# Attention one step deeper, projection heads prepared early, x's low part ahead of the angles, and attention's result read out by VectorE

## What is computed

```
q, k, v = x Wq', x Wk', x Wv'              # 32 query heads, 8 key/value heads, 128 wide
q, k = rope(rmsnorm(q)), rope(rmsnorm(k))  # positions: cache length + token
k_all = [16 cache pages of 32 keys, k];  v_all likewise   # 544 keys per sequence
p = softmax(q k_all' / sqrt(128), keys of the cache beyond its length masked)
o = p v_all;   u = o Wo'                   # 4096 -> 512
x1 = x + (causal convolution of u with a state-space kernel) + D u
out = x1 + ffn(cond(x1))                   # LoRA linear, then a gated low-rank expert layer
```

## Time and profile before

| what | value |
|---|---|
| median of 3 executions | 1270.46 us (1269.95 to 1273.42) |
| the profiled execution | 1272.64 us, span 1270.7 us |
| PE busy | 1234.1 us, 97% |
| PEld, DVE, ACT, POOL busy | 81%, 64%, 64%, 59% |
| mean granted clock of TensorE | 0.999 |
| attention of the two halves | about 166 to 482 us and 797 to 1113 us |

### The profile page before, as it was taken

One profiled execution on the slowest core, in us unless ns is written; L12 is line 12 of the kernel. 1 busy time (PEld: TensorE's weight loads), 2 busy tenths in 40 slices (PEclk: granted clock), 3 DMA queues, 4 the chain that ended last, 5 costly groups with the idle time before them and its releaser, 6 DMA issues.

```text
span 1270.7 us, 28683 instructions
## 1 busy us (share of the span) xinstructions
PE 1234.1 (97%) x7378; PEld 1033.0 (81%) x7378; DVE 810.5 (64%) x1725; ACT 809.2 (64%) x2258; POOL 753.3 (59%) x884
## 2 busy tenths in 40 slices
PE   6999999999999998999999999999999999999998
PEld 5778888899989986866777888888899998978756
DVE  5876666766766777962339766666676776655422
ACT  5676677778888874432336666778787888653320
POOL 3444467888888884433223433778888888754330
PEclk9999999999999999999999999999999999999999
DMA  6343288999999955406144242899999999434300
GB/s 229 123 134 119 96 229 227 227 232 242 237 234 234 233 139 180 145 1 199 42 161 138 96 153 90 243 217 234 226 241 239 224 234 241 108 115 145 91 32 34
DMA packets 147978, 214.82 MB, mean 169 GB/s; under 512 B 24949, under 2 KB 119479, under 8 KB 142136
## 3 DMA queue, kind: packets, MB, share of 16 engines
q1 hardware_dynamic: 130568, 204.86, 59.8%
q10 hardware_dynamic: 17328, 9.04, 2.4%
HBM read 203.33 MB, written 10.49 MB: 168 GB/s over the span
## 4 chain that ended last, share of the span: by engine, by line
PE 77%; SPq 10%; DVE 4%; issue 4%; ACT 2%; DMA 2%; ACTq 0%; DVEq 0%
PE PS L1106 14%; PE PS L1074 7%; PE PS L969 5%; PE PS L975 5%; PE PS L971 5%; PE PS L1171 4%; PE PS L1162 4%; PE PS L1168 4%; SPq L479 4%; SPq L464 4%; PE PS L1116 4%; PE PS L1213 2%; PE PS L955 2%; PE PS L1039 2%; PE PS L1041 2%
## 5 line engine op out<-in xcount | busy, mean ns | idle before, releaser
L622 POOL TENSOR_TENSOR kv_parts<-kv,k_hi 128x544 fp32r<-128x544 f32 x192 | 258.2, 1345 | 46.7 <-ACT k_hi L798 42.8
L1106 PE MATMUL PS<-probT,kv 128*128 128x128 f32 x2048 | 271.2, 275 | 5.2 <-DMA kv<-in_vpages 3.7
L1106 PEld LDWEIGHTS PS<-probT,kv 128*128 128x128 f32 x2048 | 248.8, 192 | 7.2 <-issue 5.9
L582 POOL TENSOR_TENSOR ring_parts<-ring,kv_parts 128x512 fp32r<-128x512 f32 x96 | 127.1, 1328 | 214.9 <-ACT kv_parts L685 186.8
L1594 DVE COPY probT<-PS 128x512 f32<-128x512 f32 x256 | 175.5, 686 | 3.1 <-PE PS L1074 3.1
L839 ACT ACTIVATE ring<-ring,smin 128x544 f32<-128x544 f32 x192 | 143.7, 748 | 39.4 <-DVE smin L1588 37.8
L1588 DVE CUSTOM_DVE_ANT_0 ring<-PS,mask,rq 128x544 f32<-128x544 f32 x192 | 149.8, 780 | 21.0 <-PE PS L1062 13.7
L798 ACT ACTIVATE k_hi<-kv 128x544 fp32r<-128x544 f32 x192 | 125.9, 657 | 56.8 <-PE PS L1062 50.5
L644 POOL TENSOR_TENSOR ring_parts<-ring,kv_parts 128x512 fp32r<-128x512 f32 x64 | 86.2, 1352 | 99.1 <-ACT kv_parts L894 99.1
L610 POOL TENSOR_SCALAR ring<-ring,rinv 128x512 f32<-128x512 f32 x192 | 133.3, 694 | 0.0
L1627 DVE TENSOR_TENSOR qo_parts<-qo,kv_parts 128x512 fp32r<-128x512 f32 x64 | 86.6, 1362 | 58.0 <-ACT kv_parts L896 55.2
(11 more groups left out here) (219 smaller groups left out, 2782.4 us busy)
## 6 DMA issues: line engine op xcount, KB each, us to landing
kv<-in_kpages SPq DMA_DIRECT2D x512, 128.0 KB, 2.6
kv<-in_vpages SPq DMA_DIRECT2D x512, 128.0 KB
ring<-in_w SPq DMA_DIRECT2D x44, 1024.0 KB, 5.1
v_new<-kv ACTq DMA_DIRECT2D x16, 256.0 KB, 4.3
k_new<-kv ACTq DMA_DIRECT2D x16, 256.0 KB, 2.3
kv<-k_new SPq DMA_DIRECT2D x32, 128.0 KB, 2.4
kv<-v_new SPq DMA_DIRECT2D x32, 128.0 KB
kv<-in_xT SPq DMA_DIRECT2D x8, 256.0 KB, 5.2
```

Of the source, the lines that this page charges most:

```text
L622: nc.gpsimd.tensor_tensor(kbuf_lo(par)[:, :, g, :], kbuf(par)[:, :, g, :], k_hi[:, e % 2, :].rearrange("p (j t) -> p j t", t=PSIZE), ALU.s ...
L1106: mm = nc.tensor.matmul(PS[:, at:at + D], vbuf(bpar)[:, c, gg * D:(gg + 1) * D], probT[:, g % 2, c * P:(c + 1) * P], start=(c == 0 and a = ...
```

## The change

Four edits, in five engines' streams.
- Attention's order gets one step deeper: `turn_probs` of g-3 and `values` of g-4 in step g, `turn_new` in steps 2 and 6, `values_new` in steps 0 and 4 of the next group, `v_free` in step 5 instead of 4, and the tail of the half accordingly. `spread_new` moves to steps 2 and 6.
- `keep_o` moves from ScalarE (steps 0, 4) to VectorE (steps 2, 6), and in the tail behind the last probT copies.
- The first two weights of the projection of the result and its first two heads are split by ScalarE around the last `spread_new`; the first 16 heads wait for one `keep_o` fewer. Weight block 14 is loaded before the last `o_done`, ahead of the small vectors.
- `prologue` is cut into `positions` and `angles`, and x's last low part is made between them. PE no longer waits for the sine ahead of block 1, but for the angles ahead of its tile 2 and for the sine ahead of tile 3 (their banks). On ScalarE the sine moves behind the stores of two value tiles and half of block 2, the rest of which now stands ahead of the first squares, in both halves.

```
 load_w(h, 15)
+sp.wait_ge(new_turned, QUADS * (h + 1))
+load_w(h, 14)                                  # was behind the small vectors
 sp.wait_ge(o_done, QUADS * (h + 1))
...
+for m in range(2, TILES): store_v(0, m)        # ScalarE, was behind the sine
+for c in range(2): upper(2, c)
 with act.If(h < 1):
     act.wait_ge(ang_ready, 1)
     ... Sin, Sin
+for c in range(2, KC): upper(2, c)
 for n in range(KU):
-    upper(2 + n // TILES, n % TILES)
+    if n >= TILES: upper(3, n % TILES)
     squares(n)
...
-if g % GU == 1 and not (first and g < GU):     # ScalarE, attention step
+if g % GU == 2 and not (first and g < GU):
     spread_new(b if g > GU else b - 1, int(g < GU))
-if g % GU == 0 and not first:
-    keep_o(b - 1, g // GU)
...
+upper_w(0); upper_w(1); upper_o(0)             # ScalarE, end of attention
 spread_new(HB - 1, 1)
+upper_o(1)
...
-pe.wait_ge(trig_ready, 2)                      # PE, ahead of block 1
...
-if g == GU and not first: mm.then_inc(v_free, 1)
+if g == GU + 1 and not first: mm.then_inc(v_free, 1)
...
 scores(b, par, g, first)                       # PE, attend
-if not (first and g < 2): turn_probs(b, g - 2, first); turn_new at g == 5, 1
+if not (first and g < 3): turn_probs(b, g - 3, first); turn_new at g == 6, 2
-if not (first and g < 3): values(b, par, g - 3, first)
+if not (first and g < 4): values(b, par, g - 4)
-if g == 7: values_new(b, par, 0, first)
-elif g == 3 and not first: values_new(b - 1, 1 - par, 1, False)
+if g == 0 and not first: values_new(b - 1, 1 - par, 0)
+elif g == 4 and not first: values_new(b - 1, 1 - par, 1)
...
 lower_x(0, range(3))                           # VectorE
-prologue()
+positions()
 lower_x(0, range(3, KC))
+angles()
...
-dve.wait_ge(pt_ready, s - 1)                   # VectorE, attention step
-V.tensor_copy(probT[:, g % 2, :], bank(4)).then_inc(pt_main, 1)
+dve.wait_ge(pt_ready, s - 2)
+V.tensor_copy(probT[:, (g - 3) % 2, :], bank(4)).then_inc(pt_main, 1)
...                                             # behind the reciprocal of the step
+if g % GU == 2 and not first:
+    keep_o(b - 1, g // GU)
+def keep_o(b, u):
+    dve.wait_ge(o_done, h * QUADS + b * UNITS + u + 1)
+    V.tensor_copy(qo[:, ds(b * (HQ * SEQ) + u * GU * D, GU * D)], bank(6 + u)).then_inc(ot_read, 1)
```

More of the change, by code:

```diff
@@ L761, in _ @@
                     nc.scalar.activation(gain[:, 0:1], dls[:, 1:2], ACT.Exp, scale=-1.0).then_inc(gain_ready, 1)
+                for m in range(2, TILES):
+                    store_v(0, m)
+                for c in range(2):
+                    upper(2, c)
+                with act.If(h < 1):
                     act.wait_ge(ang_ready, 1)
@@ L881, in _, with upper_w @@
                     step(HB - 1, 1, g, False, True)
[L882 to L888, removed]
+                def upper_w(head):
                     n, a = head // 4, head % 4
@@ L895, in _, with upper_o @@
                         .then_inc(whi_ready, 1)
-                    nc.scalar.activation(ohi[:, a, :].rearrange("p (b t) -> p b t", b=HB),
-                                         oT[:, :, head, :], ACT.Copy).then_inc(ohi_ready, 1)
+                def upper_o(head):
+                    if head == 0:
+                        act.wait_ge(ot_read, QUADS * (h + 1) - 1)
+                    if head == HQ // 2:
+                        act.wait_ge(ot_read, QUADS * (h + 1))
+                    nc.scalar.activation(ohi[:, head % 4, :].rearrange("p (b t) -> p b t", b=HB),
+                                         oT[:, :, head, :], ACT.Copy).then_inc(ohi_ready, 1)
+                upper_w(0)
+                upper_w(1)
+                upper_o(0)
+                spread_new(HB - 1, 1)
+                upper_o(1)
+                for head in range(HQ):
+                    if head >= 2:
+                        upper_w(head)
+                        upper_o(head)
                     if head == 7:
@@ L1051, in scores @@
                     mm = nc.tensor.matmul(PS[:, at:at + mid], q_hi[:, u, q], hi[:, 0:mid], start=True, stop=False)
-                    if g == GU and not first:
+                    if g == GU + 1 and not first:
                         mm.then_inc(v_free, 1)
@@ L1086, in turn_new, with values @@
                     nc.tensor.transpose(PS[:, 2560:2688], prob_new[:, u, :], ident).then_inc(new_turned, 1)
-                def values(b, par, g, first):
+                def values(b, par, g):
                     s = h * STEPS + b * HK + g
@@ L1108, in values, with values_new @@
                     mm.then_inc(pv_done, 1)
-                def values_new(b, par, u, first):
-                    if first and u == 0:
+                def values_new(b, par, u):
+                    if isinstance(b, int) and b == 0 and u == 0:
                         pe.wait_ge(spread_clear, h + 1)
@@ L1121, in attend @@
                         scores(b, par, g, first)
-                        if not (first and g < 2):
-                            turn_probs(b, g - 2, first)
-                            if g == 5:
+                        if not (first and g < 3):
+                            turn_probs(b, g - 3, first)
+                            if g == 6:
                                 turn_new(b, 0, first)
-                            elif g == 1:
+                            elif g == 2:
                                 turn_new(b - 1, 1, False)
[L1128 to L1133, removed]
+                        if not (first and g < 4):
+                            values(b, par, g - 4)
+                        if g == 0 and not first:
+                            values_new(b - 1, 1 - par, 0)
+                        elif g == 4 and not first:
+                            values_new(b - 1, 1 - par, 1)
                 scores(0, 0, 0, True)
@@ L1322, in prologue, with angles @@
                 link(V.tensor_scalar(pos, pos, con("seqpos"), None, ALU.add))
+            def angles():
                 a3 = ang.rearrange("p (m f) -> p m f", m=HALVES * TILES)
@@ L1621, in _ @@
                 step(HB - 1, 1, HK + 1, False)
+                keep_o(HB - 1, 0)
+                step(HB - 1, 1, HK + 2, False)
+                keep_o(HB - 1, 1)
                 def lower(head):
```

47 lines of the change are left out of this document (26 added, 21 removed).

## The result

| | before | after |
|---|---|---|
| median, us | 1271.94 (4 runs, 1269.95 to 1279.29) | 1296.76 (4 runs, 1294.92 to 1297.92) |
| ratio to before, 95% interval | | 1.0181 [1.0161, 1.0202] |
| profiled execution, span | 1272.6, 1270.7 | 1297.9, 1295.9 |

The forecast was 1290 (1274 to 1301), a sum of +19.2 us; the spans of the two profiled executions differ by +25.2.

A forecast was written before the change was run, and what follows sets the result against it. TensorE, busy nearly all of the span, was taken as the bound. The terms -5.0 + 23.8 - 0.2 + 0.8 - 3.2 + 3.0 gave +19.2 us, put on the median of 1270.46: 1290 us, range 1274 to 1301.

The forecast's parts named there:

- keep_o on VectorE: Attention: the copy adds 0.72 us to VectorE's step, TensorE waits 0.41 us in each of 58 groups, +23.8 us.
- s + 6.61: Attention: TensorE reaches the next group's step-0 transposes 6.61 us after s, the end of step 1's scores; allowed from s + 7.02.
- The deeper order: Attention: value pages are needed one step later, so the waits for them go in both halves, -5.0 us.
- The front, first half: Before the first attention: 4.9 us freed at TensorE's stop return as idleness ahead of the first transpose, -0.2 us.
- Second half: Second half's front: no stall to remove, first squares 1.7 us later, partly given back, +0.8 us.
- The ends: From attention's last values_new to the first product with olo: idle 1.4 us instead of 3.0 a half, -3.2 us.
- The drain's +3.0: End of each attention half: transposes wait 1.17 us for the copy, other waits add 0.3; 1.5 a half, +3.0 us.
- Weight block 14: First projection: its load goes ahead of the small vectors VectorE's second head needs; 0 to 3 us, taken as 0.
- no stall: Attention: keep_o adds less than 0.31 us, so TensorE never waits for step-0 transposes; 1266 us, chance 0.15.
- half a stall: Attention: the copy overlaps its neighbours better, adding about 0.5 us, 0.2 a stall, 12 us; 1278 us, chance 0.11.
- the front kept: Front: its 4.9 us are kept if VectorE and ScalarE finish key units equally sooner; with the stall 1285 us, chance 0.11.
- Rival 4: Attention: step 3's transposes, with 0.12 us to spare, stop too, +0.2 us in each of 58; 1301 us, chance 0.06.

The follow-up runs named there:

- x1: The changed kernel with keep_o back on ScalarE, in steps 1 and 5; ratio to the kernel before 0.9952.
- x7: x1 with the ends put back as in the kernel before; ratio to the kernel before 1.0005.
- x8: The kernel before, in its old order, with keep_o on VectorE in steps 0 and 4; ratio to the kernel before 1.0170.
- x4: The changed kernel with keep_o ahead of the reciprocal, still on VectorE in steps 2 and 6; ratio to the kernel before 0.9986.
- x6: x1 with the front put back as in the kernel before; ratio to the kernel before 0.9950.
- z1: x1 with VectorE's small-vector work two heads later and the front as before; 1261.59 us, ratio to the kernel before 0.9916.

## Why the forecast was right, and where its terms were off

1. *keep_o on VectorE* (+23.8, the term that decided). Right in mechanism and place: the chain of masking, copy and transposes, and a second copy that lengthens spacing and group alike by 0.52 us. Right in size too, with a mean group of +0.41 us, but by two errors that nearly cancel. The copy adds 0.64 us in the mean, where the forecast took 0.72 (the lower bound of its rows was 0.61). And the forecast counted TensorE's arrival, s + 6.61, to the modelled end of the scores, which the transposes need not wait for: by starts it is s + 6.45, so the margin at this place is 0.15 us and not 0.31. 0.64 - 0.15 is 0.49, 0.72 - 0.31 is 0.41, and the stalls measured by starts are 0.45. From x1 to the changed kernel attention grows by 25.3 us over both halves (the forecast has 23.8, and 0.72 for each of the two drains, 25.2; that it agrees so closely is luck by the same two errors).
2. *The deeper order* (-5.0). Mis-sized, and with a term put at nothing. The waits for value pages did go, but the row I took them from counts weight loads and matmuls together; TensorE's own waits for these pages were 3.7 us in 7, and the two waits of weight loads fall together with two of them. And the new order has a price at the fill that the sum left out: 1.0 and 1.8 us more of waits in the two halves, and 1.7 us of low clock in each half in the changed kernel's execution. Alone it came to 0.9991, and in the table to a gain of 1.3 us over both attentions.
3. *The front, first half* (-0.2): right to within its noise (+0.2): the 4.9 us are given back. But the forecast had them all as one stop of some 4 us ahead of the first transposes; only 2.87 are there, and 2.09 come 11 us earlier, at a bank that VectorE's rotation had not read. It also named a low clock there, and the granted clock stayed at 1.00. *Second half* (+0.8): right in kind, too small; it is +2.2 in every pair.
4. *The ends* (-3.2). Measured -2.9 on the way to olo. Right. The drain's +3.0 lies inside the attention column, and no run tells it apart. *Weight block 14* (0, up to 3): +0.4 in the first projection of the changed kernel. No run moves it alone, but nothing shows that it delays the small vectors: VectorE could start on them 6.4 us after the last values_new in x1, with the block ahead of them, and 7.6 after in x7, with the block behind. What stopped x1 is that its heads come 2.3 us sooner.
5. The rivals: no stall, half a stall and the front kept all fall. Rival 4 (the transposes of step 3 also stop) did not happen in the changed kernel as a second stall, but its margin of 0.1 us was real: it is the one that x8 ran into.

By terms: attention +25.4 where the forecast had -5.0 + 23.8 + 3.0 = 21.8, the second front 1.4 more than forecast, the rest 1.0 more together. The missed 6 us are 3.6 + 1.4 + 1.0. The windows at the fill point to the deeper order's term for the first; they give more than 3.6, though, so part of the drain's +3.0, which no run tells apart, may not have been there. That split is argued, not shown.

## What to carry to other kernels

On an engine that does its work in order and feeds another once a step, an eviction's price is not its share of busy time but where it stands: put ahead of an operation that has to wait anyway it added nothing to the step (x4), put behind it it cost 0.41 us in each of 58 groups. So before moving work, write down for each step by how much the slow engine is ready before the fast one asks (here 0.1 us at step 3 and 0.15 at step 0), counting from start to start, since the idle time in the brackets leaves out what two matmuls overlap, and see which step the move shifts, all the way round the loop. And when a wait is taken out, look at what follows it in order: sooner heads ran into the load of the small vectors, and a pause of 2.8 us then cost more again in clock than in waiting.

## What the runs showed of the hardware

- VectorE's copy of 128x512 from PSUM holds its successor for 0.61 us (415.69 to 416.30) of its 0.69. Behind a reciprocal that is waited for it began 0.21, 0.41, 0.31 or 0.33 us after that one began, in turn from group to group; behind another copy, 0.60 after that one began, with no gap. The forecast's estimate of 0.66 us held was worked out from the overhead of about 125 ns that the Trainium skill, "Perfetto Trace Analysis", Optimizing Scalar/DVE Operations, gives for VectorE on PSUM; the trace has 0.61. The gap in front, which that overhead doesn't hold, decides as much.
- TensorE's clock after a pause: in x1 it was busy 1.22 of 4 us (488 to 492) and then ran at a granted 0.50, 1.2 GHz, for over 4 us; in the changed kernel it was busy 1.13 of 4 us (42 to 46), with a stop of 2.87, and the clock stayed at 1.00, as it did behind a pause of 1.6 us ahead of the first olo. So two stretches of 4 us with nearly the same work were followed by different clocks. At the first half's fill (174 to 182 us) it fell in eight of the ten kernels of the deeper order (in the second half in four), and in none of the four of the old one; which of two kernels with the same front and fill it hits can't be told beforehand (x6 not, z1 yes).
